# A hand-ordered four-layer transformer kernel: every engine's list of steps rewritten, and waits for counts already passed left out

## What is computed

```python
# block 0, attentions 0 (causal, on itself) and 1 (on ctx), 16 heads; lengths from the count of nonzero energies
x1 = ln(x + mha(x, x, causal));  x2 = ln(x1 + mha(x1, ctx));  x = ln(x2 + fc2(relu(fc1(x2))))
# block 1, attention 2: q from ln(x), k and v from ln(ctx), 16 heads
x = x + softmax(q k / sqrt(8)) v @ Wo + bo;  x = x + silu(x @ W1 + b1) @ W2 + b2
# block 2, attentions 3 (causal) and 4 (on ctx), pre-norm, then relu feed-forward 128-512-128
# block 3, attentions 5, 6, 7: 4 heads, relu on q, k, v, absent keys and queries masked
for i in range(3): enc = ln_unbiased(mha(q, k, v) + q); enc = leaky_relu(enc @ Wff + bff) + enc
```

## Time and profile before

| | before |
|---|---|
| median of 3 runs | 1001.06 us (1000.65 to 1001.94) |
| the profiled execution: its own time | 1002.01 us |
| its span, first to last instruction | 1000.0 us |
| mean granted clock of TensorE | 0.985 |
| PE busy | 904.4 us |
| DVE, ACT, POOL busy | 780.6, 606.3, 321.4 us |

### The profile page before, as it was taken

How to read it: one execution, slowest core, us unless ns; L and a number is a source line. 1 busy time by engine, 2 the same in 40 slices (tenths; PEclk the granted TensorE clock), 3 DMA queues, 4 the chain that set the end, 5 groups by cost and what they waited for, 6 DMA issues and landing times.

```text
span 1000.0 us, 42125 instructions
## 1 busy us (share of the span) xinstructions
PE 904.4 (90%) x18602; PEld 657.6 (66%) x18602; DVE 780.6 (78%) x2202; ACT 606.3 (61%) x890; POOL 321.4 (32%) x389
## 2 busy tenths in 40 slices
PE   8788898799998999989899889979999989998886
PEld 4466666477676776666666666756767676766654
DVE  4799999985668575888779998987776675578787
ACT  5356776567867655445565575747777766444542
POOL 4023344520111123455642322634111111246543
PEclk9899999999999999999999998989999999999999
DMA  8000000000000000000000000000000000000001
GB/s 274 2 24 21 7 3 3 1 2 4 2 3 3 3 13 12 24 3 3 13 24 14 3 3 3 4 2 2 4 2 3 3 4 2 3 2 3 2 3 44
DMA packets 13733, 13.69 MB, mean 14 GB/s; under 512 B 617, under 2 KB 13170, under 8 KB 13298
## 3 DMA queue, kind: packets, MB, share of 16 engines
q1 hardware_dynamic: 13554, 11.00, 3.5%
HBM read 8.91 MB, written 2.10 MB: 11 GB/s over the span
## 4 chain that ended last, share of the span: by engine, by line
PE 28%; DVE 19%; POOL 4%; ACT 3%; issue 2%; POOLq 0%; ACTq 0%
PE pair L720 6%; DVE mx L1408 4%; PE pair L958 3%; PE pair L793 3%; PE pair L977 3%; PE pair L707 2%; PE pair L953 2%; DVE stats L1131 2%; PE pair L826 2%; DVE Y L1205 2%; DVE X L1286 2%; PE pair L991 1%; DVE Y L1154 1%; PE pair L714 1%; ACT PT L1053 1%
## 5 line engine op out<-in xcount | busy, mean ns | idle before, releaser
L1053 ACT ACTIVATE PT<-pair 128x1024 f32<-128x1024 f32 x184 | 184.5, 1025 | 120.4 <-PE pair L958 85.9
L1408 DVE TENSOR_REDUCE mx<-pair 128x16 f32<-128x1024 f32 x184 | 218.8, 1216 | 45.4 <-PE pair L958 37.7
L720 PE MATMUL pair<-xf,W_all 128*128 128x512 f32 x336 | 175.0, 621 | 4.4 <-ACT xf L1019 2.5
L1435 POOL TENSOR_SCALAR ve<-mv 128x4 f32<-128x4 f32 x64 | 17.0, 265 | 434.0 <-DVE mv L1134 433.9
L958 PEld LDWEIGHTS pair<-KQ 32*128 32x128 f32 (+1 forms) x3840 | 108.4, 158 | 24.3 <-issue 3.9
L958 PE MATMUL pair<-KQ 32*128 32x128 f32 (+1 forms) x3840 | 119.9, 255 | 4.0 <-DVE Y L1154 1.2
L1019 ACT ACTIVATE KQ<-pair,c 128x512 f32<-128x512 f32 x160 | 101.3, 689 | 32.0 <-PE pair L720 31.5
L1019 ACT ACTIVATE KQ<-pair,cols 128x512 f32<-128x512 f32 x120 | 81.2, 691 | 43.0 <-PE pair L720 42.8
L1019 ACT ACTIVATE V<-pair 64x512 f32<-64x512 f32 x128 | 79.4, 621 | 39.7 <-PE pair L826 37.9
L977 PE MATMUL pair<-PT,V 128*32 128x64 f32 x5120 | 93.8, 222 | 6.6 <-ACT PT L1053 3.0
L977 PEld LDWEIGHTS pair<-PT,V 128*32 128x32 f32 x5120 | 78.1, 111 | 29.9 <-issue 13.4
(11 more groups left out here) (126 smaller groups left out, 1689.8 us busy)
## 6 DMA issues: line engine op xcount, KB each, us to landing
W_all<-weights SPq DMA_DIRECT2D x1, 2880.0 KB, 13.9
Xin<-x SPq DMA_DIRECT2D x8, 256.0 KB, 2.9
C<-ctx SPq DMA_DIRECT2D x8, 256.0 KB, 4.0
out<-X SPq DMA_DIRECT2D x8, 256.0 KB, 2.5
row<-rows SPq DMA_DIRECT2D x1, 1024.0 KB, 7.3
c<-const SPq DMA_DIRECT2D x1, 390.0 KB, 5.7
W_all<-weights SPq DMA_DIRECT2D x1, 192.0 KB, 3.0
c<-const SPq DMA_DIRECT2D x1, 93.0 KB, 2.0
```

The lines of the kernel that those rows point to most:

```text
L720: pe.matmul(t[:, 0:TOK], W(name), src[:], start=True, stop=True).then_inc(*banks.full(*use))
L1053: act.activation(PT[:, place, :], banks.of("B", a, s, v)[:], ACT.Exp, scale=float((D // (2 * PAIRS[a])) ** -0.5)).then_inc(*banks.drain((" ...
L1408: dve.tensor_reduce(dst, banks.of("A", a, s, v)[:].rearrange("p (u m t) -> p u m t", u=2, t=S), AX.X, ALU.max).then_inc(*banks.drain(("A", ...
```

## The change

All five lists of `ORDER` are written anew. The same 1152, 752, 829, 176 and 16 steps are in them; their order, the PSUM places, the `PT` buffers and the places of the fillings are others (30 places, 73 fillings). One line of PE's list before, and what begins the list now:

```diff
-        pq@0; 0.2.1 maxrow@2+5; 0.2.2 A0@30; 0.2.1 B0@13; 0.3.0 down@5; 0.2.1 B1@01 v0@4 v1; 0.2.3 q@5; 0.2.1 v2@0
+        0.0.0 x@0; 0.0.1 x@1+8; 0.0.0 pq@0 pk@1; 0.0.3 x@2+5; 0.0.1 pq@3; 0.0.2 x@0; 0.0.0 first@1; 0.0.3 pv@2; 0.0.0
```

Each engine's waits go through an object that remembers the highest count it has waited for on each semaphore, and the exponentials count on `operand` instead of a semaphore of their own:

```diff
+class Once:
+
+
+    def __init__(self, engine):
+        self.engine, self.passed = engine, {}
+
+    def wait_ge(self, sem, count):
+        if self.passed.get(sem.num, 0) < count:
+            self.passed[sem.num] = count
+            self.engine.wait_ge(sem, count)
...
-    def take(self, pe, places, width, *uses):
+    def take(self, once, places, width, *uses):
...
-            pe.wait_ge(self.sems[sem], count)
+            once.wait_ge(self.sems[sem], count)
...
-        probs = sig("probs")
...
-                        pe.wait_ge(*operand.at("x1", a, s))
+                        once.wait_ge(*operand.at("x1", a, s))
...
-                    pe.wait_ge(*probs.at(a, s, v))
+                    once.wait_ge(*operand.at("probs", a, s, v))
...
-                                       ).then_inc(*banks.drain(("B", a, s, v), probs, a, s, v))
+                                       ).then_inc(*banks.drain(("B", a, s, v), operand, "probs", a, s, v))
```

More of the change, by code:

```diff
@@ L52 @@
     "PE": """
[L53 to L72, removed]
@@ new lines @@
+        v3; 0.0.2 A1@20; 0.0.1 B0@13; 0.0.0 t1@4; 0.0.2 maxrow@5+1; 0.0.1 B1@01 v0@4 v1; 0.0.3 A1@30; 0.0.1 v2@5 t0@4
+        v3; 0.0.2 B0@13; 0.1.0 x1@5; 0.0.1 t1@4; 0.0.3 maxrow@0; 0.0.2 v0@1; 0.1.0 kv@5 pq@2 pv@3; 0.0.2 v1; 0.1.0
+        pk@2; 0.0.3 B0@23; 0.0.2 t0@0; 0.1.0 first@1; 0.0.3 B1@13; 0.1.1 x1@0; 0.1.0 length@1; 0.0.3 v0@4 v1 v2@1;
+        0.1.0 maskrow@0; 0.1.1 kv@5 pq@2 pk@3; 0.1.0 A0@23; 0.1.1 pv@0; 0.0.3 t0@2; 0.3.0 ctx@3; 0.0.3 v3; 0.1.0
+        A1@23; 0.0.2 B1@10; 0.5.0 ksum@6; 0.0.3 t1@7; 0.2.1 kv@4; 0.1.0 maxrow@5; 0.2.0 kv@6; 0.0.2 v2@2 v3; 0.1.0
@@ new lines @@
+        B0@03; 0.0.2 t1@2; 0.5.0 pv@3; 0.1.0 B1@23 v0@0 v1; 0.1.3 x1@1; 0.5.1 ksum@2; 0.1.1 first@3; 0.1.0 v2@1 t0@0;
+        0.1.1 length@2; 0.1.0 v3; 0.1.2 x1@3; 0.2.0 pv@4; 0.1.3 kv@1; 0.1.2 pq@3; 0.1.1 maskrow@0; 0.1.3 pq@2 pv@1
+        pk@3; 0.1.2 kv@2; 0.5.2 ksum@4; 0.2.0 pk@5; 0.1.1 A0@03; 0.1.2 pv@2; 0.1.3 first@3; 0.1.1 A1@02; 0.1.2 pk@6;
+        0.1.3 length@7; 0.5.3 ksum@2; 0.1.0 t1@3; 0.2.2 kv@7; 0.1.3 maskrow@0; 0.3.1 ctx@1; 0.1.2 first@6; 0.1.1
+        maxrow@1; 0.5.1 pv@0; 0.1.1 B0@23; 0.1.2 length@0; 0.5.0 maskrow@1; 0.1.2 maskrow@0; 0.1.1 B1@13 v0@1 v1;
@@ new lines @@
+        0.7.1 x@3+1; 0.6.3 maskrow@0; 0.7.2 ff@1; 0.6.3 A0@1; 0.7.1 ksum@0 pk@4 pq@1; 0.7.2 x@5; 0.7.1 maskrow@0;
+        0.6.3 maxrow@4; 0.7.1 pv@2; 0.7.2 ksum@1; 0.6.3 B0@2; 0.7.1 A0@0; 0.7.2 maskrow@2; 0.8.0 x1@3; 0.7.2 pk@6;
+        0.6.3 v0@3 v1@7; 0.7.1 maxrow@2; 0.7.2 pq@6 pv@3 A0@0; 0.7.1 B0@2; 0.8.0 ff@2; 1.0.0 x@3; 0.7.2 maxrow@0;
+        0.7.1 v0@1 v1@2; 1.0.0 pv@0 pq@1; 0.7.3 x1@2; 0.7.2 B0@2; 0.7.3 ff@0; 1.0.0 pk@1; 0.7.2 v0@0 v1@2; 0.7.3
+        x@3+1; 1.0.0 first@0; 0.7.3 pv@1 ksum@0; 0.8.1 x1@2; 1.0.0 length@3; 0.7.3 pk@4 pq@1 maskrow@0; 0.8.1 ff@2;
@@ new lines @@
+        1.1.0 maxrow@3; 1.1.1 first@4; 1.2.1 kv@0; 1.1.0 B0@13; 1.1.1 length@0; 1.3.1 ctx@1; 1.1.0 B1@23; 1.1.1
+        maskrow@0; 1.1.0 v0@1 v1; 1.1.2 kv@2; 1.2.0 pk@0; 1.1.2 pv@2; 1.1.1 A0@23; 1.1.3 x1@3; 1.3.2 ctx@0; 1.1.0
+        t0@1; 1.1.1 A1@12; 1.1.0 v2@0; 1.1.2 pk@6; 1.1.3 pq@7; 1.2.2 kv@1; 1.1.0 v3; 1.1.2 first@6; 1.1.1 maxrow@7;
+        1.5.0 ksum@0; 1.1.0 t1@2; 1.1.3 kv@1; 1.1.1 B0@23; 1.1.2 length@0; 1.1.3 pv@1; 1.1.1 B1@13; 1.1.2 maskrow@0;
+        1.1.1 v0@4 v1; 1.1.3 pk@1; 1.3.3 ctx@0; 1.1.2 A0@13; 1.1.1 v2@5 v3; 1.1.2 A1@01; 1.1.1 t0@4; 1.1.3 first@5;
@@ L687, in fill @@
                     loaded(pool, "warm")
-                    held.update(zip(uses, banks.take(pe, places, width, *uses), strict=True))
+                    held.update(zip(uses, banks.take(once, places, width, *uses), strict=True))
                     for _ in range(n):
```

705 lines of the change are left out of this document (354 added, 351 removed).

## The result

The changed kernel takes **970.12 us** (median of 4 runs, 969.08 to 971.18); the kernel before took 1000.86 beside it (1000.16 to 1001.94). The profiled execution took 969.08 us for a span of 967.1, at a mean granted clock of 0.991.

A forecast was written before the change was run, and what follows sets the result against it. PE, busy 904.4 of 1000.0 us, was taken as the limit, with DVE as much so in five stretches. Waits 5, order 7.5 and clock 3 sum to 15.5 us less than 1001.06: 986 us, range 975 to 1003.

The forecast's parts named there:

- more is gained: Rival, chance 0.10: the new order brings 15 us and the clock 7, so about 973 us.
- term two: New order of steps: fewer PE steps close behind the one whose result they need; 7.5 us less, bounds 0 and 15.
- Term one: PE loses 814 wait-only instructions; a late separate wait costs 0.09 us more; 5 us less, bounds 0 and 6.3.
- The rule that the prediction set against this term: PE pulls weight loads ahead of matmuls under way, so late separate waits would cost nothing and the waits' gain be 0.
- 16 kinds: Turnarounds such as `maxrow` to `B0` or `length` to `maskrow`, priced 0.72, 0.16, 0.09 us with none, one, two steps between.
- PE's work itself doesn't change: On PE: same steps, 73 fillings for 74, so at most its 95.6 us of idle time can be gained.
- Term three: Stretches at 0.50 granted clock follow gaps over 1 us, and some go; 3 us less, bounds 0 and 10.2.
- DVE's stretches absorb it: Rival, chance 0.18: in five 50 us stretches DVE's chain sets the pace, 40% of waits' and order's gain goes, 995 us.
- DVE busy the same 780 us: Sign to look for in the profile: DVE's busy time stays 780 us, and so becomes a larger share.

The follow-up runs named there:

- the two kernels with some 900 separate waits: Changed kernel with all PE's real waits sent as separate instructions, 977.14 us; changed kernel with a spare passed separate wait before each waiting PE step, 970.67 us.
- the kernel put closer: Changed kernel with 16 places of PE's list edited so that nothing stands between a step and the one that needs its result: 979.59 us, ratio 0.980.
- the cut kernel: Kernel before, old waits, all lists old up to the old order's 368.7 us (416 PE steps) and new from there: 978.44 us, ratio 0.980.

## Why the prediction was too small

**Direction held.** Both parts of the change gain, separate waits on PE are 226, gaps fell to 60.7 us (65 forecast), the clock is 0.99, most late matmuls follow their releaser by 0.06 us. What came is the rival "more is gained" (973, to which 0.10 was given), and term two went beyond its bound of 15. PE is the fullest engine, but that it alone sets the end is not what the profile shows; of the chain that ended last, by engine, in the changed kernel:

```profile
PE 43%; DVE 43%; ACT 6%; POOL 3%; issue 2%; DMA 1%; SPq 1%; POOLq 0%; DVEq 0%; ACTq 0%
```

The clock has fallen to 0.50 in three stretches, leaving out the start's and the last 2 us.

```profile
31.80:38.62 6.82, 6.82 (x92) 4.77 (x96) 4.69 (x13) 0.00 (x0) 0.00 (x0) 0.50 0.01 2
99.97:103.40 3.43, 3.33 (x57) 2.77 (x59) 3.29 (x16) 1.19 (x2) 1.26 (x2) 0.51 0.00 0
161.50:164.90 3.40, 3.40 (x45) 2.58 (x34) 3.25 (x8) 1.20 (x2) 1.75 (x2) 0.50 0.03 5
956.80:960.20 3.40, 3.40 (x13) 2.04 (x12) 1.25 (x4) 1.20 (x2) 0.00 (x0) 0.50 0.16 50
```

The windows are laid over these four stretches of the changed kernel; PE is busy 16.95 us of 17.05 in them.

**Term one, the waits: 5 forecast, 9 to 10 measured on the old order.** The mechanism and its 0.09 us held, and so did the size, as far as the waits themselves go: without the clock they bring 3.6 to 4.3 us on the old order, within the bounds of 0 and 6.3. What the term left out is that a kernel with other waits has another clock: 5.3 to 6.1 us, by the table of the experiments. The single traces say it less clearly: with the new waits the span is 10.1 us shorter, 3.7 of that by the clock (PE busy 18.6 us at 0.50 instead of 26.0), which leaves 6.4, and gaps ahead of steps are only some 1.5 of these. On the new order 103 late separate waits become 46: 57 x 0.09 = 5.1, against 4.8 measured without the clock. The rule that the prediction set against this term would, as it was read there, make the two kernels with some 900 separate waits equal, and they are 6.5 us apart. But the Trainium skill (TensorE: Matmul & The Clock Gate, section Step-by-step: what each phase is for) speaks of weight loads pulled ahead of matmuls under way, and ahead of a late step none is under way: what the runs refute is that reading, not what the Trainium skill says.

**Term two, the order: 7.5 forecast, 25 measured, 20.5 of them without the clock.** This is the step that failed: the gaps were priced by the number of steps between, and only for 16 kinds; all other waits, and the last matmul ahead of a gap, were put at nothing. The gaps by number of steps between, for the same 16 kinds, and the forecast; "new order" is the kernel with the old waits, so that nothing else differs:

| steps between | before | new order | forecast | came |
|---|---|---|---|---|
| none | 9, 6.4 us | 3, 1.7 us | -4.3 | -4.7 |
| one | 69, 11.0 | 57, 4.2 | -1.9 | -6.8 |
| two | 123, 11.2 | 109, 9.2 | -1.3 | -2.0 |
| all other steps | 51.5 | 46.7 | 0 | -4.8 |
| all | 80.1 | 61.8 | -7.5 | -18.3 |

The price with nothing between is right (0.72; 0.70 in the kernel put closer). With one step between, the price itself halved, 0.16 to 0.07. A number of steps isn't a length, since the step between may be a `maskrow` of 0.2 us or a `down` of over 3; that this is what halved the price is not shown. The waits ahead of `x` and `x1`, with POOL's affine part in them, the second group of the earlier trace rows, were never among the kinds: 9.2 us in 18 before, 5.8 in 11 in the new order. To these 18.3 us of gaps come some 6 for the last matmuls of steps that were followed by a gap, which "PE's work itself doesn't change" priced at nothing, and 0.9 of the clock in these two traces: some 25 for a span 26.0 shorter.

What it was in the new order that let DVE deliver earlier was not isolated: only whole parts of all lists were exchanged. Shown is where it gained (23.4 of 26.0 us in the trace behind step 416, confirmed by the cut kernel), and that eight gaps closed in PE's list alone don't give it: they got 1.8 us of gaps for 7.9. The new places in PSUM and of the `PT` buffers are part of the order, and no run has them by themselves.

**Term three, the clock: 3 forecast, 4.5 by the table above.** Near enough, but in part by luck. The clock belongs to no part of the change: the order alone has 4.7 of it over its executions (0.9 in its one trace), the waits alone 5.3 to 6.1, both together 5.4. And that falls go with the gaps of over 1 us is not borne out: the trace of the changed kernel has 20 such gaps and the one before 17, with fewer falls in the changed one. A filling does not buy it back either: without the 73, 5.7 us more are lost at 0.50 and 8.6 us of PE's work saved.

**DVE's stretches.** The rival "DVE's stretches absorb it" was right for the first of them: PE's steps 46 to 190 take 115.1 us before (58.8 to 173.9) and 118.8 after, which is the same but for the clock (3.4 us), and DVE idles 6.4 and 4.1 us there. It was wrong for the second, where 10.2 us were gained: 6.8 by the clock, which the rival put at nothing, and 3.3 by the rest. DVE had idled 16.7 us between steps 585 and 783, more than the 4.5 of 600 to 650, and now idles 6.8. I had taken idle time by stretches of 50 us, and it lay beside them.

**DVE busy the same 780 us** was wrong, it is 791.3; below.

## What to carry to other kernels

Price a wait by whether it is late, not by its number: some 700 more waits for passed counts cost nothing here, and 0.09 us each was lost where the late wait was not the one that the matmul carries. A gap's price works in one direction: a consumer put next to its producer costs the 0.7 us that the trace shows for such places, but the same gap closed in one engine's list comes back further on unless the other engine's list is moved with it, so judge a new order by equal work between points that both orders pass, and add to each gap the last matmul ahead of it. And take the clock's cost off before you compare: here eight edits made a kernel 5 us faster that is 2.5 us slower without the clock.
